# Cross-attention and routed FFN on one core: the last FFN rearranged (half of the output product ahead, ranks from the PSUM bank, keys and queries in two banks, end of the program reordered)

## The chip, the cores and the metric

The kernel runs on one core of a Trainium2 chip. The metric is the device time of one execution in microseconds. Three executions of the kernel before gave 905.43, 905.71 and 909.38 us; their median is 905.71 us. A further execution was recorded with the hardware profiler: 908.64 us, of which 906.5 us are the span from its first to its last instruction. All times inside the span below are counted from the span's start in that one execution.

The engines are named as in the profile: PE is TensorE (matmuls), PEld its weight loads, DVE is VectorE, ACT is ScalarE, POOL is GpSimd, SP is SyncE. Each engine runs its own instruction list in order, and engines meet at semaphores.

## The reference

```python
B, S, D = 8, 512, 256                      # samples, tokens, width; context of 1024 tokens; 16 heads of 16
x = x + cross_attention(layernorm(x), ctx, mask)          # ends with  out @ w_o.T
y = layernorm(x)
scores = y @ w_router
idx = top_k(scores, 128)                                  # 128 of the 512 tokens of each sample
x_sel = y[idx]
h = rmsnorm(x_sel, g1);  q, k, v = split(h @ W_qkv.T)     # 16 heads of 16
x_attn = causal_softmax(q k^T / 4) v @ W_out.T
h2 = rmsnorm(x_sel + x_attn, g2)
x_ff = (silu(h2 @ W1.T) * (h2 @ W2.T)) @ W3.T             # inner width 682
out = x + y.at[idx].set(x_sel + x_attn + x_ff)
```

The output is therefore `x + y` for every row, and for the 128 chosen rows `x_attn + x_ff` is added on top.

## The kernel before

The eight samples are a software pipeline. In the loop over `b`, each of the 32 steps (`STEPS`) of sample `b` is one pair of score products, one pair of exponentials on ACT and one set of value products; the FFN of sample `b - 1` and the projections of sample `b + 1` are put between the steps by tables (`PE_SLOT`, `ACT_SLOT`, `DVE_ORDER`). All of these use one PSUM bank, `MISC` (7), for everything that is not attention.

The FFN of the last sample has nothing to hide behind. It runs after the loops, by the lists `PE_FFN`, `ACT_FFN`, `DVE_FFN` and `POOL_FFN`, with its PSUM banks from `BANK_LAST`. It is one dependent chain that crosses the engines. In order: `wo0`, `wo1` (output product of cross-attention, PE; residual sum and layernorm statistics, DVE), `var` (POOL: reciprocal root of the variance), `y` (DVE: four normalised tiles, then four scores), `spread` (PE lays the 512 scores along every partition; ACT copies them to `all_scores` in SBUF), `rank0` to `rank3` (DVE counts for each token how many scores lie ahead of it and builds the selection matrix `sel`), `gather` (PE multiplies `sel` with `y`; DVE takes the rows, squares them, scales them by POOL's `rms0`), `hidT` (PE transposes, ACT copies), `kq` and `v` (PE; DVE and ACT copy), `fs` (scores, PE; exponentials, ACT), `causal` (POOL), `pv`, `wout`, `hid2T`, then `u0`, `w0`, `u1`, `w1` (four products of 48 matmul records each, with ACT's tanh and DVE's two multiplications per half), and `down:0`, `down:1` with DVE's last sum `att`. POOL's stage `add` (L775 to L784) then adds the 128 rows to the output in DRAM with one indirect DMA.

Between the stages of this chain PE is given products that nobody reads, `spare_products`, in the numbers of `SPARE` (L88): they multiply the constant bf16 tile `before` with 512 columns and write an unused bank. They stand in PE's list ahead of the stage that they are named after, so that stage's matmuls can start only when its spare products are through.

`base = x1 + y` (L674) is made by DVE after `gather`, and SP stores it (L242). POOL's `add` waits for that store (L779) because it adds onto it. A `check` of all denominators of the softmaxes goes into `checks`; PE sums it over the partitions (`flag`), and DVE turns it into `flags_i`. Two operations of that check (L980 to L985) stand between `y` and `rank0` in DVE's list.

The program has two blocks. The first ends when all five engines have arrived (the profile puts these instructions at L803). SP arrives only after `wait_ge(added, 16 * B)` (L858), and POOL only after waiting for the last indirect DMA (L783). In the second block, whose body runs only if the check failed, each engine loads `flags_i`, branches over the body, and meets the others once more (L1071); with that the program ends.

## Time and profile before

| what | value |
|---|---|
| median of 3 executions (lowest, highest) | 905.71 us (905.43, 909.38) |
| profiled execution | 908.64 us |
| its span | 906.5 us |
| PE busy | 868.0 us (96%), 12039 matmul records |
| ACT busy | 570.1 us (63%) |
| DVE busy | 317.3 us (35%) |
| POOL busy | 93.1 us (10%) |
| mean granted TensorE clock | 0.995 of full speed |

Shares over the span tell of the seven steady rounds. The change lies in the last 70 us, where each engine mostly waits for another one, so the table's shares say little about it; the order of events in time is what is to be read. PE's busy time there also holds the spare products.

### The profile page before, as it was taken

The numbers are of one execution on the slowest core, as the hardware profiler recorded it, in microseconds if no ns is written. First come the engines' busy times: TensorE is split into PE (matmuls) and PEld (weight loads), VectorE is DVE, ScalarE is ACT, GpSimd is POOL, SyncE is SP. The second block draws the span as 40 slices with busy tenths as digits, with TensorE's granted clock in tenths as the row PEclk, the third lists the DMA queues.
The fourth block names the chain that finished last, engine by engine and source line by source line (L and its number), as shares of the span: only waits on it lengthen the run. The fifth ranks groups of instructions, "written<-read, shape, count | busy, mean of one in ns | idle before, by whom it ended". The sixth has DMA issues, their size and how long they took to land. (4 is left out here: it accounts for less than half of the span.)

```text
span 906.5 us, 28692 instructions
## 1 busy us (share of the span) xinstructions
PE 868.0 (96%) x12039; PEld 304.9 (34%) x12039; DVE 317.3 (35%) x919; ACT 570.1 (63%) x645; POOL 93.1 (10%) x147
## 2 busy tenths in 40 slices
PE   7999999999999999999999999999999999999974
PEld 2322232333333423334323433334323432323443
DVE  3122126331553217331453316442363314421631
ACT  3566767666676767666676666766676667776010
POOL 4000101110100101011000101011101100010010
PEclk9999999999999999999999999999999999999998
DMA  5060200120011200111001200101001000100000
GB/s 180 32 209 1 77 3 25 49 77 8 3 33 40 78 8 25 48 56 28 5 25 49 78 7 25 49 17 63 8 2 48 31 8 2 48 2 9 1 24 9
DMA packets 25226, 33.73 MB, mean 37 GB/s; under 512 B 1246, under 2 KB 22024, under 8 KB 25096
## 3 DMA queue, kind: packets, MB, share of 16 engines
q1 hardware_dynamic: 23944, 30.81, 10.6%
q0 software_dynamic: 1152, 1.05, 1.0%
q8 instruction: 98, 1.61, 0.7%
q14 instruction: 32, 0.26, 0.1%
HBM read 26.61 MB, written 5.24 MB: 35 GB/s over the span
## 5 line engine op out<-in xcount | busy, mean ns | idle before, releaser
L470 ACT ACTIVATE probs<-pair_bank 128x1024 f32<-128x1024 f32 x512 | 496.2, 1021 | 237.7 <-ACTq L469 237.7
L440 PE MATMUL pair_bank<-q_sb,k_sb 32*64 32x512 f32 x4096 | 285.9, 613 | 8.6 <-PEq L437 8.5
L459 PE MATMUL o_bank<-probs,va 128*32 128x512 f32 x2048 | 272.9, 604 | 1.4 <-ACT probs L470 1.1
L459 PEld LDWEIGHTS o_bank<-probs,va 128*32 128x32 f32 x2048 | 41.5, 108 | 205.1 <-issue 116.4
L440 PEld LDWEIGHTS pair_bank<-q_sb,k_sb 32*64 32x64 f32 x4096 | 61.0, 130 | 141.2 <-issue 141.2
L543 DVE STREAM_TRANSPOSE o_blk<-o_bank 128x512 f32<-128x512 f32 x32 | 22.9, 717 | 138.2 <-DVEq L542 138.2
L256 PE MATMUL m_bank<-wv_sb,ctx_in 128*32 128x256 f32 x1024 | 61.5, 380 | 0.0
L256 PE MATMUL m_bank<-ctx_in,wk_sb 128*32 128x512 f32 x480 | 60.3, 592 | 0.0
L585 DVE TENSOR_SCALAR va<-m_bank,valid 128x256 f32<-128x256 f32 x64 | 28.1, 479 | 63.6 <-DVEq L582 63.4
L256 PEld LDWEIGHTS m_bank<-hid_t,w 128*32 128x32 f32 x1392 | 39.3, 110 | 17.3 <-issue 16.7
L256 PEld LDWEIGHTS m_bank<-wv_sb,ctx_in 128*32 128x32 f32 x1024 | 33.1, 110 | 34.6 <-issue 19.3
L256 PE MATMUL m_bank<-hid_t,w 128*32 128x128 f32 x1392 | 43.4, 273 | 0.5 <-PEq L271 0.5
L266 PE MATMUL o_bank<-before 128*128 128x512 bf16 x120 | 30.7, 414 | 2.7 <-POOL before L864 2.7
L256 PE MATMUL m_bank<-xn_t,wq_sb 128*32 128x512 f32 x240 | 29.6, 592 | 0.0
L772 POOL TENSOR_SCALAR_AFFINE_SELECT p_f<-p_f 128x1024 f32<-128x1024 f32 x16 | 17.5, 1091 | 116.4 <-POOLq L770 115.3
L756 POOL TENSOR_TENSOR mask_in<-mask_in,mask_row 128x256 int32<-128x256 int32 x32 | 22.4, 729 | 68.4 <-POOLq L753 68.4
L781 POOL DMA_INDIRECT out_dram<-att,row_of x8 | 13.3, 1668 | 152.2 <-POOLq L780 152.2
L596 DVE TENSOR_SCALAR q_sb<-m_bank,parity 128x512 f32<-128x512 f32 x15 | 11.3, 750 | 47.1 <-DVEq L595 47.1
L256 PEld LDWEIGHTS m_bank<-ctx_in,wk_sb 128*32 128x32 f32 x480 | 15.7, 110 | 35.9 <-issue 35.9
L616 DVE TENSOR_TENSOR x<-x,m_bank 128x512 f32<-128x512 f32 x14 | 9.6, 687 | 50.9 <-DVEq L615 50.9
L789 POOL TENSOR_SCALAR ms<-ms 128x1 f32<-128x1 f32 x16 | 3.1, 191 | 235.6 <-POOLq L788 235.6
L256 PE MATMUL m_bank<-wo,o_t 128*32 128x256 f32 x448 | 26.7, 379 | 0.0
(166 smaller groups left out, 623.8 us busy)
## 6 DMA issues: line engine op xcount, KB each, us to landing
ctx_in<-in_ctxT SPq DMA_DIRECT2D x7, 1024.0 KB, 5.0
x_in<-in_x SPq DMA_DIRECT2D x8, 512.0 KB, 4.0
x<-in_x SPq DMA_DIRECT2D x8, 512.0 KB, 4.4
mask_in<-in_mask SPq DMA_DIRECT2D x8, 512.0 KB, 3.9
out_dram<-base SPq DMA_DIRECT2D x8, 512.0 KB, 5.3
ctx_in<-in_ctxT SPq DMA_DIRECT2D x2, 512.0 KB, 7.1
mask_row<-in_mask SPq DMA_DIRECT2D x8, 128.0 KB, 3.9
wqkv<-in_wqkvT SPq DMA_DIRECT2D x1, 768.0 KB
```

The lines of the kernel that those rows point to most:

```text
L256: last = nc.tensor.matmul(dst[j], a[:, j], c, start=(begins and n == 0), stop=(ends and n == len(pairs) - 1))
L266: last = nc.tensor.matmul(dst, before[:, 0, 0:P], before[:, 1], start=True, stop=True)
L440: last = nc.tensor.matmul(pair_bank[pairs[r // 2]][j:j + 64, r % 2], key_tile(b, s, r)[:, j:j + 64], query_tile(b, s, r), start=True, stop ...
L459: last = nc.tensor.matmul(o_bank[32 * r:32 * r + 32], va[b % 2][:, t, HV * h:HV * h + 32], probs[s % 2][:, r], start=(t == 0), stop=(t == ...
L470: nc.scalar.activation(probs[s % 2][:, 2 * e:2 * e + 2, :], pair_bank[p][:], ACT.Exp, scale=HD ** -0.5).then_inc(s_free[p], 1)
L543: nc.vector.transpose(o_blk[:], o_bank[:]).then_inc(o_free, 1)
L585: last = nc.vector.tensor_scalar(by_head(va[b % 2][:, t])[:, :, 0:HD], bank[i][:, e * D:(e + 1) * D].rearrange("p (h d) -> p h d", h=H), o ...
L596: nc.vector.tensor_scalar(q_sb[b % 2][:, m, 0], bank[i], parity[:, 0:1], None, ALU.mult).then_inc(q_sb_ready, 1)
L616: nc.vector.tensor_tensor(x1[:, 2 * pr:2 * pr + 2], x1[:, 2 * pr:2 * pr + 2], bank[i].rearrange("p (t d) -> p t d", t=2), ALU.add).then_in ...
L756: last = nc.gpsimd.tensor_tensor(mask_words[:, t * WORDS:(t + 1) * WORDS], mask_words[:, t * WORDS:(t + 1) * WORDS], first, ALU.subtract)
L772: last = nc.gpsimd.affine_select(out=half, in_=half, compare_op=ALU.is_ge, fill=0.0, base=0, pattern=[[0, H8], [1, CAP]], channel_multipli ...
L781: nc.gpsimd.indirect_dma_start(out.rearrange("b s d -> (b s) d"), bass.IndirectOffsetOnAxis(row_of[:, 0:1], 0), att[:], None, compute_op=A ...
```

## The change

The lists of the last FFN are rewritten and six things change.

1. `wo`: the output product of the last sample is made in four banks, one for each tile of 128 tokens. Its first half (the heads whose transposed output `o_t[:, 0]` is there early) runs before the last attention group is normalised, the second half after. DVE adds each tile as it comes. `SPARE` ahead of it falls from 12 to 2, and these go to bank 4.
2. `y` becomes `score`: the mean is subtracted while POOL makes the reciprocal root; the scores are made with the root as the scalar factor; `y` itself is multiplied with the root after the scores have been handed on.
3. `spread` goes to bank 4, and `rank0` to `rank3` read it there. ACT's copy to `all_scores` is gone from this FFN. `SPARE` falls from 24 to 15 ahead of `spread` and from 36 to 25 ahead of `gather`.
4. The check of the denominators moves behind `gather` on DVE (`check all`), and `base` behind the keys and queries, so the store is issued later.
5. `k,q`: keys go to one bank and queries to the next, so DVE can take the keys while PE makes the queries. `u1` is put ahead of `w0`.
6. The end: POOL waits for `base_stored` before `delta_ready`, and no longer for its own last indirect DMA; SP's wait for `added` moves from the end of the first block to the second block, behind the load of `flags_i`.

```diff
-BANK_LAST = {"wo0": 0, "wo1": 1, "spread": 7, "gather": 0, "hidT": 7, "kq": 0, "v": 1, "pv": 7, "wout": 0,
+BANK_LAST = {"wo": 0, "spread": 4, "rank0": 4, "rank1": 4, "rank2": 4, "rank3": 4, "gather": 0, "hidT": 7, "k,q": 0, "v": 7, "pv": 7, "wout": 0,
...
-PE_FFN = ["wo0", "wo1", "spread", "gather", "hidT", "kq", "v", "fs", "pv", "wout", "hid2T", "flag", "u0", "w0", "u1",
+PE_FFN = ["wo", "spread", "gather", "hidT", "k,q", "v", "fs", "pv", "wout", "hid2T", "flag", "u0", "u1", "w0",
           "w1", "down:0", "down:1"]
-ACT_FFN = ["spread", "hidT", "v", "fs", "hid2T", "u0", "u1"]
-DVE_FFN = ["wo0", "wo1", "y", "rank0", "rank1", "rank2", "rank3", "gather", "base", "kq", "pv", "wout", "check", "u0", "w0", "u1", "w1",
+ACT_FFN = ["hidT", "v", "fs", "hid2T", "u0", "u1"]
+DVE_FFN = ["wo", "score", "rank0", "rank1", "rank2", "rank3", "gather", "check all", "k,q", "base", "pv", "wout", "check", "u0", "u1", "w0", "w1",
...
-SPARE = {"wo0": 12, "spread": 24, "gather": 36, "hidT": 10, "pv": 14, "wout": 6, "hid2T": 10}
+SPARE = {"wo": 2, "spread": 15, "gather": 25, "hidT": 10, "pv": 14, "wout": 6, "hid2T": 10}
...
         def pe_ffn(pe, stage, i, part=None):
+            if stage == "wo":
+                pe.wait_ge(o_t_ready, 1)
+                tiles = [take_bank(pe, i + t)[:, 0:D] for t in range(QT)]
+                for t in range(QT):
+                    product(tiles[t], [(o_t[:, 0, t * P:(t + 1) * P], wo[:, 0])], ends=False)
+                pe.wait_ge(o_t_ready, 2)
+                pe.sem_inc(o_t_ready, -2)
+                for t in range(QT):
+                    product(tiles[t], [(o_t[:, 1, t * P:(t + 1) * P], wo[:, 1])], begins=False).then_inc(done["wo"], 1)
...
+            elif stage == "k,q":
+                pe.wait_ge(hidT_sb, 1)
+                pe.sem_inc(hidT_sb, -1)
+                for e in range(2):
+                    dst = take_bank(pe, i + e)
+                    for n in range(2):
+                        first = (D if e == 0 else 0) + n * P
+                        last = product(dst[:, n * CAP:(n + 1) * CAP],
+                                       [(wqkv[:, c, first:first + P], hid_t[:, c]) for c in range(KC)])
+                    last.then_inc(done["kq"], 1)
...
         def dve_ffn(dve, stage, b, i):
+            if stage == "wo":
+                dve.wait_ge(xres_in, 16)
+                dve.sem_inc(xres_in, -16)
+                for t in range(QT):
+                    dve.wait_ge(done["wo"], 1)
+                    dve.sem_inc(done["wo"], -1)
+                    nc.vector.tensor_tensor(x1[:, t], x1[:, t], bank[i + t][:, 0:D], ALU.add).then_inc(bank_free[i + t], 1)
+                    dve.drain()
+                    nc.vector.bn_stats(stats2[:, t], x1[:, t])
+                dve.drain()
+                for t in range(QT):
+                    nc.vector.bn_aggr(mv2[:, t], stats2[:, t])
+                dve.drain().then_inc(var2_ready, 1)
+            elif stage == "score":
+                for t in range(QT):
+                    nc.vector.tensor_scalar(y[:, t], x1[:, t], mv2[:, t, 0:1], None, ALU.subtract)
+                dve.wait_ge(rstd2_ready, 1)
+                dve.sem_inc(rstd2_ready, -1)
+                dve.drain()
+                for t in range(QT):
+                    unused = ties[t // 2][:, (t % 2) * D:(t % 2 + 1) * D]
+                    nc.vector.scalar_tensor_tensor(out=unused, in0=y[:, t], scalar=rstd2[:, t:t + 1], in1=wr_b[:], op0=ALU.mult,
+                                                   op1=ALU.mult, accum_out=score[:, t:t + 1])
+                dve.drain().then_inc(score_ready, 1)
+                for t in range(QT):
+                    nc.vector.tensor_scalar(y[:, t], y[:, t], rstd2[:, t:t + 1], None, ALU.mult)
...
             elif stage in ("rank0", "rank1", "rank2", "rank3"):
                 t = int(stage[4])
-                if t == 0:
+                others = all_scores[:] if i == MISC else bank[i]
+                if t == 0 and i == MISC:
                     dve.wait_ge(all_ready, 1)
                     dve.sem_inc(all_ready, -1)
+                elif t == 0:
+                    dve.wait_ge(done["spread"], 1)
+                    dve.sem_inc(done["spread"], -1)
...
+                    if i != MISC:
+                        dve.sem_inc(bank_free[i], 1)
...
+            elif stage == "k,q":
+                dve.wait_ge(done["kq"], 1)
+                dve.sem_inc(done["kq"], -1)
+                nc.vector.tensor_copy(k_f[:], bank[i][:, 0:D].rearrange("p (m k) -> p m k", m=M2)).then_inc(bank_free[i], 1)
+                dve.wait_ge(done["kq"], 1)
+                dve.sem_inc(done["kq"], -1)
...
+            elif stage == "check all":
+                nc.vector.tensor_scalar(ties[0][:], inv_all[:].rearrange("p n c -> p (n c)"), DEN_LOW, None, ALU.is_ge)
+                dve.drain()
+                nc.vector.scalar_tensor_tensor(out=ties[0][:], in0=inv_all[:].rearrange("p n c -> p (n c)"), scalar=DEN_HIGH,
+                                               in1=ties[0][:], op0=ALU.is_le, op1=ALU.mult, accum_out=checks[:, 0:1])
+                dve.wait_ge(mask_free, 1)
+                nc.vector.tensor_reduce(checks[:, 1:2], differs[:], op=ALU.add, axis=AX.X)
...
             elif stage == "add":
+                pool.wait_ge(base_stored, 16)
+                pool.sem_inc(base_stored, -16)
                 pool.wait_ge(delta_ready, 1)
                 pool.sem_inc(delta_ready, -1)
-                pool.wait_ge(base_stored, 16)
-                pool.sem_inc(base_stored, -16)
                 nc.gpsimd.indirect_dma_start(out.rearrange("b s d -> (b s) d"), bass.IndirectOffsetOnAxis(row_of[:, 0:1], 0),
                                              att[:], None, compute_op=ALU.add).then_inc(added, 16)
-                pool.wait_ge(added, 16 * (n + 1))
-                pool.sem_inc(add_done, 1)
+                if n != B - 1:
+                    pool.wait_ge(added, 16 * (n + 1))
+                    pool.sem_inc(add_done, 1)
...
                 store(sp, B - 1)
-                sp.wait_ge(added, 16 * B)
...
                 general = sp.value_load(flags_i[0:1, 0:1], min_val=0, max_val=1)
+                sp.wait_ge(added, 16 * B)
                 with sp.If(general == 1):
...
                 with pool.If(general == 1):
+                    pool.wait_ge(added, 16 * B)
+                    pool.sem_inc(add_done, 1)
```

## Rows read from the trace of the kernel before

**Rows 1.** By stretch: length; busy of PE, PEld, DVE, ACT, POOL; PE clock; DMA.

```profile
837.00:896.00 59.00, 48.95 (x610) 26.59 (x602) 25.68 (x78) 5.38 (x10) 4.92 (x8) 0.97 0.03 10
```

**Rows 2.** Timeline, output product to statistics: start us, length us, engine, line, operation.

```profile
839.51 0.71 DVE L552 STREAM_TRANSPOSE o_t<-o_nrm 128x512 f32<-128x512 f32 x1
840.53 3.66 PE L256 MATMUL pair_bank<-wo,o_t 128*32 128x256 f32 x64
842.63 0.69 DVE L616 TENSOR_TENSOR x<-x,pair_bank 128x512 f32<-128x512 f32 x1 [2.41 <-DVEq L615]
843.41 0.75 DVE L620 BATCH_NORM_STATS2 stats<-x 128x6 f32<-128x256 f32 x2
...
845.96 0.38 DVE L624 BATCH_NORM_AGGREGATE mv<-stats 128x2 f32<-128x6 f32 x4
...
847.04 1.05 POOL L766 TENSOR_TENSOR rstd<-veps,neg_half 128x4 f32<-128x4 f32 x1 [0.24 <-issue]
```

**Rows 3.** Timeline, normalisation, scores, spread and ranks.

```profile
848.23 1.38 DVE L630 TENSOR_SCALAR y_tok<-x,mv,rstd 128x256 f32<-128x256 f32 x4 [1.90 <-DVEq L628]
849.69 0.43 DVE L634 SCALAR_TENSOR_TENSOR ties<-y_tok,wr_b 128x256 f32<-128x256 f32 x1
...
851.49 0.62 PE L247 MATMUL m_bank<-ident,score 128*128 128x128 f32 x4 [2.02 <-PEq L271]
...
852.24 0.60 ACT L497 ACTIVATE all_scores<-m_bank 128x512 f32<-128x512 f32 x1 [14.63 <-ACTq L496]
...
853.03 0.35 DVE L644 SCALAR_TENSOR_TENSOR ties<-all_scores,score,before 128x128 f32<-128x128 f32 x1 [0.43 <-DVEq L641]
...
857.82 0.77 DVE L606 TENSOR_SCALAR sel<-iota_r,rank 128x128 f32<-128x128 f32 x2
```

**Rows 4.** Groups by form on DVE, one operation from SBUF and one from PSUM: count, busy us, mean ns.

```profile
L647 DVE SCALAR_TENSOR_TENSOR ties<-all_scores,score,before 128x384 f32<-128x384 f32 x1 | 0.6, 617 | 0.0
...
L717 DVE SCALAR_TENSOR_TENSOR silu<-half_tanh,pair_bank 128x384 f32<-128x384 f32 x1 | 0.6, 555 | 1.4 <-DVEq L716 1.4
```

**Rows 5.** Timeline of PE: spare products ahead of spread, ahead of gather, and gather.

```profile
844.12 5.35 PE L266 MATMUL o_bank<-before 128*128 128x512 bf16 x24
...
851.95 9.62 PE L266 MATMUL o_bank<-before 128*128 128x512 bf16 x36
861.50 1.95 PE L256 MATMUL pair_bank<-y_tok,sel 128*32 128x257 f32 x32
```

**Rows 6.** Busy time by stretches of 1 us around the ranks, columns as in Rows 1.

```profile
852.00:853.00 1.00, 1.00 (x7) 0.38 (x5) 0.60 (x3) 0.60 (x1) 0.00 (x0) 0.83 0.00 0
853.00:854.00 1.00, 1.00 (x4) 0.42 (x3) 0.97 (x4) 0.00 (x0) 0.00 (x0) 0.50 0.00 0
...
856.00:857.00 1.00, 1.00 (x6) 0.49 (x5) 0.93 (x6) 0.00 (x0) 0.00 (x0) 0.97 0.00 0
```

**Rows 7.** Timeline, base, keys and queries.

```profile
866.39 1.23 DVE L674 TENSOR_TENSOR base<-x,y_tok 128x1024 f32<-128x1024 f32 x1
...
867.85 1.96 PE L256 MATMUL pair_bank<-hid_t,wqkv 128*32 128x128 f32 x64 [0.84 <-PEq L271]
...
869.97 0.42 DVE L680 COPY k_f<-pair_bank 128x256 f32<-128x256 f32 x1 [2.36 <-DVEq L679]
870.32 0.87 DVE L682 TENSOR_SCALAR q_f<-pair_bank,parity 128x256 f32<-128x256 f32 x2
```

**Rows 8.** Timeline of PE, rest of the four inner products.

```profile
889.45 3.15 PE L256 MATMUL pair_bank<-hid_t,w 128*32 128x128 f32 x107 [0.78 <-issue]
```

**Rows 9.** Timeline, the last sum and the indirect DMA.

```profile
895.52 0.42 DVE L739 TENSOR_TENSOR att<-att,pair_bank 128x256 f32<-128x256 f32 x1 [1.87 <-DVEq L738]
...
896.89 1.66 POOL L781 DMA_INDIRECT out_dram<-att,row_of  x1 [12.97 <-POOLq L780]
```

**Rows 10.** DMA issues after 895 us: engine, count, us to landing.

```profile
out_dram<-att,row_of POOLq DMA_INDIRECT x1, 3.8
```

**Rows 11.** Waits of SP's queue at the end: total us, times, longest.

```profile
SPq L1071 <- PEq L1071: 4.3, 1, 4.3
```

More of the change, by code:

```diff
@@ L676, in dve_ffn @@
                 dve.drain().then_inc(base_ready, 1)
+            elif stage == "k,q":
[4 more added lines that the diff above has]
+                dve.sem_inc(done["kq"], -1)
+                for par in range(2):
+                    last = nc.vector.tensor_scalar(q_f[:, :, par], bank[i + 1][:, 0:D].rearrange("p (m k) -> p m k", m=M2),
+                                                   parity[:, par:par + 1], None, ALU.mult)
+                last.then_inc(bank_free[i + 1], 1)
+                dve.drain().then_inc(kq_sb, 1)
             elif stage == "kq":
@@ L976, in _ @@
                 dve.drain()
[L977 to L987 removed]
+                for stage in DVE_FFN:
                     dve_ffn(dve, stage, B - 1, BANK_LAST.get(stage, MISC))
@@ L1060, in _ @@
                     if stage in SPARE:
-                        spare_products(SPARE[stage], bank[1] if stage == "wo0" else o_bank[:])
+                        spare_products(SPARE[stage], bank[4] if stage == "wo" else o_bank[:])
                     if stage == "fs":
```

19 lines of the change are left out of this document (4 added, 15 removed).

## The prediction

> **What bounds the kernel now.** I read the busy time by stretch first, then the timeline of the last 70 us engine by engine, and last what happens behind the last computing instruction. The stretch from 837 to 896 us is 59 us long and no engine but PE is near full: DVE is busy for 26 us, ACT and POOL for 5 us each [rows 1]. PE's 49 us hold 112 spare products that nobody reads. So nothing is bound by throughput here; the time is the length of one dependent chain, and only three kinds of thing shorten it: a link that is taken off the chain, a link that starts on part of its input, and a queue (PE's spare products above all) that no longer keeps a ready link waiting. The seven steady rounds before 837 us keep their instructions, except that POOL waits for two old semaphores in the other order; I cost them at nothing.
>
> The links, with their ends: the last transposed group `o_t` is there at 839.51 + 0.71 = 840.22, the output product runs from 840.53 to 844.19, DVE's first sum starts at 842.63, the statistics end at 845.96 + 0.38 = 846.34, POOL's root at 847.04 + 1.05 = 848.09 [rows 2]. Then come `y` from 848.23, the scores from 849.69, `spread` on PE at 851.49, ACT's copy at 852.24, the ranks from 853.03 to 857.82 + 0.77 = 858.59 [rows 3]. And here the chain leaves DVE: `gather` could follow 0.3 us behind its input, as the output product follows `o_t` [rows 2], so at 858.9, but it starts at 861.50, when the 36 spare products ahead of it are through [rows 5]. That is 2.6 us in which PE's own filling is the bound.
>
> **Part 1, output product (gain 0.9 us).** The first half (32 of 64 records, 3.66 / 2 = 1.83 us) goes ahead of `o_t`'s second half. A spare product takes 5.35 / 24 = 0.22 us [rows 5]; the 12 of before took 2.7 us ahead of 840.5, so PE is free from about 837.8. Two remain, then five waits of the queue; starting at about 838.4 the half ends at 840.3, just as `o_t` comes. If it were late, each 0.1 us would cost 0.1 us. From 840.5 each tile takes 0.46 us. DVE's first sum, before 2.1 us behind the start of the product [rows 2], now comes 0.46 + 0.3 us behind it, at 841.25. The load moves to DVE: a 256-wide sum is 0.42 us (the sum of `att` [rows 9]), a gap of 0.09 us as between the 512-wide sum and the statistics, 0.38 us for one tile's statistics [rows 2], and some 0.05 us for the wait: 0.93 us a tile, longer than PE's 0.46. Four tiles end at 845.0, so the statistics are complete at 845.45 instead of 846.34. Bounds: 0.7 us (0.1 us more per wait) to 1.1 us. POOL then ends at 847.2.
>
> **Part 2, mean and root apart (gain 1.45 us).** The four subtractions (1.38 us [rows 3]) run from 845.5 to 846.9, beside POOL's root, which ends at 847.2: they are covered. Without that cover they would cost up to 1.38 us again. The scores start at 847.35 and take 1.47 us as before (849.69 to 851.16), so `spread` starts near 849.15 instead of 851.49. Together with part 1 that is 2.35 us.
>
> **Part 3, ranks from the bank (gain 0.25 us).** Removed: ACT's copy with its two hand-overs, from the end of `spread` at 852.11 to 853.03, 0.9 us [rows 3]. Now `spread` ends at 849.8, and DVE could start at 850.05. But the multiplication of `y` by the root (1.38 us plus drain) sits ahead of `rank0` in DVE's queue and ends at 850.3; behind it wait the ranks, and everything behind them. So the ranks start at 850.45: 1.3 us behind `spread`'s start where it was 1.54. The two check operations that stood at this place were hidden behind ACT before and now stand behind `gather`, beside POOL's root, PE's `hidT` and the key product; they take 0.43 + 0.69 + 0.15 us by their shapes, and the `base` operation of 1.23 us that stood in this place was hidden as well [rows 7]. The eight counting operations now read PSUM. A 384-wide three-operand operation from SBUF took 617 ns, one from PSUM 555 ns [rows 4], so I charge nothing; bounds -0.3 to +0.5 us over the eight. The Trainium skill ("VectorE: DVE Perf Modes", the errata section) speaks against this edit: it gives VectorE 58 fixed cycles from SBUF and 120 from PSUM at 0.96 GHz, which by an estimate from that page would cost 8 x 65 ns = 0.5 us. The rows here show no such step, and the measurement decides. The ranks end at 850.45 + 5.56 = 856.0, 2.6 us earlier than before.
>
> **Part 4, fewer spare products (gain 2.2 us).** The clock: after PE's idle stretch from 849.47 (end of the 24 products) to 851.49 the granted clock fell to half at about 852.7 and came back at about 856.0; four products fitted into a microsecond instead of six to seven [rows 5, 6]. In the changed kernel PE has 15 spare products (3.3 us) behind the output product, which ends at 842.4, and is then idle from about 845.9 to 849.15, 3.2 us instead of 2.0: I expect the fall again, earlier. 25 products at full clock are 5.4 us, from 849.6 to 855.0; with 3.3 us of them at half clock it is 1.7 us more, 856.7. `gather` may start at 856.3. So the bound is DVE or PE by a little: I take 856.7, between 856.3 and 857.2 (the last if the half clock lasts longer). Before it was 861.50: 4.8 us in all, of which 2.6 are parts 1 to 3 and 2.2 this one.
>
> **Part 5, keys and queries (gain 0.35 us).** The product of keys and queries is 64 records, 867.85 to 869.81, 0.84 us for each half [rows 7]. DVE's copy of the keys (0.42 us, its next operation 0.35 us behind it) started at 869.97, behind the whole; now it runs beside the second half, and the queries can start at 869.97 instead of 870.32. The later `base` (1.23 us) is beside PE's scores, ACT's exponentials, POOL's masking and the value product, all ahead of DVE's next input. The store goes out 4 us later and has over 15 us left before POOL needs it; its queue on SP has nothing behind it. Bounds 0.2 to 0.4 us.
>
> **Part 6, inner products (gain 0.1 us).** PE is the bound here; 0.78 us of it is a stall inside `w0` that no wait explains [rows 8]. The other order lets DVE finish its last gate sooner, which took at most 0.2 us from PE. The Trainium skill ("Runtime: NRT & Kernel Launch", the section on instruction fetch) says that a sequencer's instructions come in blocks of 256; by that the stall would be a late block, and with 60 PE instructions fewer ahead of it, it would fall 60 instructions later, still among these products. From the rows alone I keep it, with -0.8 to +0.8 us as its bounds.
>
> **Part 7, the end (gain 2.25 us).** The last sum ends at 895.94, POOL issues from 896.89 to 898.55 [rows 9], the DMA lands 3.8 us after 896.89, at 900.7 [rows 10], and only then does the first block close; the second block takes the rest to 906.5, 5.8 us, of which SP stands 4.3 us waiting for PE's queue [rows 11]. With both waits for the DMA gone from the first block, it closes behind the issue, 900.7 - 898.55 = 2.15 us earlier. SP's wait for the landing, about 2 us behind the new close, is then hidden behind its 4.3 us of waiting for PE. The swapped waits of POOL take one wait from between 895.94 and 896.89: 0.1 us, bounds 0 and 0.2.
>
> **The sum** against the profiled execution: 0.9 + 1.45 + 0.25 + 2.2 + 0.35 + 0.1 + 2.25 = 7.5 us, 908.64 - 7.5 = 901.1. The profiled execution is 2.9 us above the median of the three timed ones. One part of the sum may be missing from these: without the fall of the clock the 36 products would end 1.7 us earlier, part 4 would shrink to 0.5 us and the sum to 5.8. No row tells how many of the timed runs had it. I go between the two, 6.8 us: 905.71 - 6.8 = 898.9.
>
> **Rivals.**
> (a) POOL's instruction list can't close the block before its DMA has left or landed. For it: no row of before shows POOL doing anything behind this DMA without an explicit wait. Against it: the engine shows 1.66 us for the DMA and no more [rows 9]. It takes back 2.15 us: 901.1.
> (b) Before's timed runs had no clock fall, and the new ones have one that makes PE late: sum 5.8 - 0.6 = 5.2 us, 900.5. For it: 2.9 us between profile and median.
> (c) Part of the chain does not shorten, because DVE is now its carrier from 841 to 856 us: 0.1 us more at each of the four tile waits, 0.5 us for PSUM reads, and a stall of 0.8 us that comes twice or at the branch into the second block. Together some 2 us: 900.9. The branch target lies elsewhere in the instruction list than before, and its price could change either way.
> (d) Slower. The longer idle of PE (3.2 us) puts the clock to half and it stays there, since the chain behind gives PE only short pieces. Three of PE's links behind the ranks, the gather (1.95 us), keys and queries (1.96 us) and the four inner products (192 records at 3.15 / 107 us, 5.65 us), are 9.5 us at full clock [rows 5, 7, 8]; at half clock these alone cost 9.5 us more, and the result would be 905.71 - 6.8 + 9.5 = 908.4 or above. It ends slower from the point where the half clock covers more than 6.8 us of these links. Against it: after the fall in the rows the clock returned within 3.3 us under spare products, and 25 of them follow here too [rows 6].
> (e) The change doesn't do what it says: the halves do not overlap, since the first half stands behind five waits, and PE's products, not DVE, set when the tiles come; then part 1 is 0.3 us and the rest stands: 899.5, inside the range.
>
> **How the numbers follow.** The forecast with its near variants, (e) among them (897 to 900.2), has 0.62; (a) 0.12; (b) and (c) together 0.17; more gain than the sum, down to 896, 0.04; (d) 0.02; and 0.03 for a mishap that leaves within 0.5%. A measurement of this kernel can tell about 0.5%, 4.5 us, from no change: faster means below 901.2. Of (a), (b) and (c) some three quarters stay below it. That gives faster 0.89, same 0.08, slower 0.03. The range holds the forecast, and (a) to (c) with their own spread: 896.3 to 902.3.
>
> **What would show it.** In the changed profile: the statistics complete near 845.45, `spread` at 849.15, the first count at 850.45 with no ACT copy ahead of it, the last selection at 856.0, `gather` within 0.6 us of it, the half clock before 854; `q_f` starting right at the end of the product; POOL's DMA near 891.5; and the span ending 7.5 us behind POOL's start instead of 9.6 (906.5 - 896.9). Part 3 is wrong if the counts are longer than 617 ns at 384 wide; part 4 if spare products still run when the ranks are done; part 7 if the distance from POOL's DMA to the end stays at 9.6 us. The whole is wrong if the granted clock is half beyond the gather.

## The result and the profile after

The changed kernel takes 902.68 us (median of 9 executions, 901.19 to 903.85). The kernel before, executed beside it, takes 907.67 us (median of 9, 905.43 to 909.38). The ratio is 0.9944, with a 95% interval of 0.9932 to 0.9957: faster by 5.0 us, or 0.56%. The forecast was 898.9 us with a range of 896.3 to 902.3. So the direction was right, the time lies outside the range, and 1.8 us of the forecast gain of 6.8 us did not come. The other 2.0 us between 898.9 and 902.68 are the level that the forecast started from: three executions of the kernel before had given 905.71, nine give 907.67.

The two profiled executions are 908.64 and 902.56 us, with spans of 906.5 and 900.6 us. To compare them I count from the moment at which the last transposed group `o_t` is complete, 840.22 us before [rows 2] and 839.03 + 0.71 = 839.74 in the changed kernel. That removes 0.48 us that came from the unchanged rounds. In the twelve traces of this study, whose rounds have the same instructions, this moment lies between 839.64 and 841.02 us, so the rounds alone move an execution by over a microsecond.

The timeline of the changed kernel; columns as in [rows 2]:

```profile
839.03 0.71 DVE L572 STREAM_TRANSPOSE o_t<-o_nrm 128x512 f32<-128x512 f32 x1
...
844.23 0.38 DVE L640 BATCH_NORM_AGGREGATE mv<-stats 128x2 f32<-128x6 f32 x4
...
844.78 1.14 DVE L645 TENSOR_SCALAR y_tok<-x,mv 128x256 f32<-128x256 f32 x4 [0.17 <-issue]
844.85 0.38 POOL L836 TENSOR_SCALAR veps<-mv 128x4 f32<-128x4 f32 x1 [11.17 <-POOLq L835]
845.46 1.11 POOL L838 TENSOR_TENSOR rstd<-veps,neg_half 128x4 f32<-128x4 f32 x1 [0.24 <-issue]
846.76 0.49 DVE L651 SCALAR_TENSOR_TENSOR ties<-y_tok,rstd,wr_b 128x256 f32<-128x256 f32 x1 [0.84 <-DVEq L647]
...
848.81 0.62 PE L247 MATMUL pair_bank<-ident,score 128*128 128x128 f32 x4 [3.64 <-PEq L271]
...
849.27 7.25 PE L266 MATMUL o_bank<-before 128*128 128x512 bf16 x25
849.92 0.35 DVE L696 SCALAR_TENSOR_TENSOR ties<-pair_bank,score,before 128x128 f32<-128x128 f32 x1 [0.18 <-DVEq L693]
...
854.71 0.77 DVE L626 TENSOR_SCALAR sel<-iota_r,rank 128x128 f32<-128x128 f32 x2
...
856.44 1.95 PE L256 MATMUL pair_bank<-y_tok,sel 128*32 128x257 f32 x32
...
864.92 0.88 DVE L738 TENSOR_SCALAR q_f<-pair_bank,parity 128x256 f32<-128x256 f32 x2 [0.45 <-DVEq L736]
...
891.18 1.66 POOL L853 DMA_INDIRECT out_dram<-att,row_of  x1 [12.64 <-POOLq L852]
```

In distances from `o_t`, with the gain summed up to each link:

| link | before | changed | gain so far | forecast |
|---|---|---|---|---|
| statistics complete | 6.12 | 4.87 | 1.25 | 0.9 |
| POOL's root | 7.87 | 6.83 | 1.04 | 0.9 |
| `spread` starts | 11.27 | 9.07 | 2.20 | 2.35 |
| ranks start | 12.81 | 10.18 | 2.63 | 2.6 |
| ranks end | 18.37 | 15.74 | 2.63 | 2.6 |
| `gather` starts | 21.28 | 16.70 | 4.58 | 4.8 |
| `q_f` starts | 30.10 | 25.18 | 4.92 | 5.15 |
| POOL's DMA issue | 56.67 | 51.44 | 5.23 | 5.35 |
| end of the span | 66.28 | 60.86 | 5.42 | 7.5 |

The first link gained 0.35 us more than forecast; from POOL's root down to the last but one line the forecast holds to a quarter of a microsecond. Then, between POOL's issue and the end, 0.2 us were gained where 2.15 had been expected: 906.5 - 896.9 = 9.6 us before, 900.6 - 891.2 = 9.4 us changed. The place is seen by asking for the instructions of the line at which the first block closes. Columns: line, queue, operation and count; length in ns; start in us. First the changed kernel, then the kernel before:

```profile
L876 SPq DRAIN  x1: 128/128/128, 868.3 to 868.3; - x1
...
L876 POOLq DRAIN  x1: 4222/4222/4222, 890.9 to 890.9; - x1
L876 DVEq DRAIN  x1: 19/19/19, 891.2 to 891.2; - x1
```

```profile
L803 SPq COMPARE_BRANCH  x1: 38/38/38, 900.7 to 900.7; - x1
L803 POOLq DRAIN  x1: 130/130/130, 900.8 to 900.8; - x1
```

At the close of the block every queue has a drain. POOL's was 0.13 us long before, standing behind an explicit wait for the DMA. In the changed kernel it is 4.22 us long and ends at 890.9 + 4.2 = 895.1, and the DMA lands 3.9 us behind its issue at 891.18, at 895.1:

```profile
out_dram<-att,row_of POOLq DMA_INDIRECT x1, 3.9
```

The explicit waits were taken out, and the drain that had always stood behind them does the same waiting.

### The profile page after: what moved, and what is told of

Same layout as the page of the kernel before. It is cut to its first block and busy times, and to the rows that moved or that the text cites. A ratio compares the mean times of both kernels' runs of the same rounds, so it can differ in the third digit from the quotient of the medians.

```text
span 900.6 us, 28635 instructions
## 1 busy us (share of the span) xinstructions
PE 860.4 (96%) x12003; PEld 300.9 (33%) x12009; DVE 318.8 (35%) x925; ACT 569.5 (63%) x644; POOL 93.3 (10%) x147
## 3 DMA queue, kind: packets, MB, share of 16 engines
q0 software_dynamic: 1152, 1.05, 1.0%
## 5 line engine op out<-in xcount | busy, mean ns | idle before, releaser
L266 PE MATMUL o_bank<-before 128*128 128x512 bf16 x95 | 25.7, 426 | 3.3 <-POOL before L936 2.7
```

The costliest lines, as they stand in the source:

```text
L266: last = nc.tensor.matmul(dst, before[:, 0, 0:P], before[:, 1], start=True, stop=True)
```

## The experiments

Times below are medians; each kernel was timed beside the kernel before, and "ratio" is to that, with its 95% interval. The kernel before itself had medians of 907.67 us beside the changed kernel, 907.42 beside four experiments (the end put back, the DMA behind the first block, 30 spare products, 25 in the kernel before), 906.72 beside four others (ranks from the copy, mean and root together, keys and queries in one bank, both edits together) and 906.55 beside the last two (the second DMA, scores before the root). So a distance to the changed kernel can differ by up to 1.1 us between medians and ratios, and a total that differs by less than that shows nothing by itself; the traces then have to carry the reading. Distances are from `o_t`, as above.

**The end put back.** In the changed kernel, only the waits of part 7 put back (POOL's two waits ahead of the DMA stay swapped):

```diff
-                if n != B - 1:
-                    pool.wait_ge(added, 16 * (n + 1))
-                    pool.sem_inc(add_done, 1)
+                pool.wait_ge(added, 16 * (n + 1))
+                pool.sem_inc(add_done, 1)
...
                 store(sp, B - 1)
+                sp.wait_ge(added, 16 * B)
...
-                sp.wait_ge(added, 16 * B)
                 with sp.If(general == 1):
...
-                    pool.wait_ge(added, 16 * B)
-                    pool.sem_inc(add_done, 1)
```

> The changed kernel with its end put back: POOL waits for its last indirect DMA again and SP's wait for it stands in the first block. Theory T (in the changed kernel the closing drain on POOL waits for the DMA's landing, 4.2 us long in the trace, so taking out the explicit waits bought nothing): the distance from POOL's DMA issue to the end of the span is 9.4 to 9.7 us, as in both kernels so far (9.57 before, 9.38 changed), and the time is that of the changed kernel, 902.7, within 0.5 us. POOL's drain is short again, 0.2 us or less, and stands behind the landing. Rival R1 (removing the waits did save 2 us, and something else in the second block took it back, such as a longer branch): the distance grows to 11.4 us or more and the time to about 904.8.

Measured: 902.47 us (901.79 to 904.99, 6 executions), ratio 0.9949 (0.9931 to 0.9967), beside 902.68 for the changed kernel. From POOL's issue at 890.68 to the end at 900.4 it is 9.7 us, 0.3 us more than in the changed kernel. The drain is short again and stands behind the landing:

```profile
L875 POOLq DRAIN  x1: 130/130/130, 894.6 to 894.6; - x1
```

So theory T holds: taking the waits out, as part 7 does, is worth 0.2 to 0.3 us in the traces and nothing that can be timed, and the second block took nothing back.

**The DMA behind the first block.** If the drain of the first block is what waits, the DMA must be issued behind it.

```diff
-                for stage in POOL_FFN:
+                for stage in POOL_FFN[:-1]:
                     pool_ffn(pool, stage, B - 1)
...
+                pool_ffn(pool, "add", B - 1)
                 general = pool.value_load(flags_i[0:1, 0:1], min_val=0, max_val=1)
```

> The changed kernel with POOL's last stage (its two waits and the indirect DMA) moved behind the meeting of the first block, ahead of POOL's load of the flag. Theory T: the first block now closes when DVE has written the flag, about 1.3 us behind the last sum; the DMA is issued there, 1.66 us, and lands 3.9 us after its start, while the other engines load the flag and branch, 5.1 to 5.4 us. The end then comes about 5.3 us behind DVE's last drain instead of 9.4 us behind POOL's issue: 3.6 to 4.0 us less than the changed kernel, near 898.9. POOL's drain at the end of the second block shows the wait for the landing. Rival R1 (the second block has a price of its own for whatever runs beside it): at most 1 us less, 901.7 or above.

Measured: 899.1 us (898.59 to 899.9, 6 executions), ratio 0.9908 (0.9892 to 0.9924). Its slowest execution is below the fastest of the changed kernel (901.19); the medians differ by 3.6 us, the lower end of what was expected. The timeline, then the drain of the second block and SP's waits (us in total, times, longest):

```profile
892.68 1.66 POOL L853 DMA_INDIRECT out_dram<-att,row_of  x1 [13.21 <-POOLq L852]
```

```profile
L1133 POOLq DRAIN  x1: 2870/2870/2870, 893.7 to 893.7; - x1
...
L1133 PEldq DRAIN  x1: 79/79/79, 896.8 to 896.8; - x1
```

```profile
SPq L1223 <- DMA out_dram<-att,row_of: 4.0, 1, 4.0
SPq L1133 <- PEq L1133: 0.4, 1, 0.4
```

The DMA is issued 1.1 us later behind the last sum than in the changed kernel, and still the end comes 4.5 us behind the issue instead of 9.4. POOL's drain ends at 893.7 + 2.9 = 896.6, the DMA lands at 892.68 + 3.9 = 896.6, and PE's drain, behind its branch, stands at 896.8. The two waits now lie beside each other and end together: SP waits 4.0 us for the DMA and then only 0.4 us for PE, where it had waited 4.3 us for PE alone [rows 11].

**A second DMA in front of the drain.** The same trace pattern would come from a drain that waits a fixed time behind an issue. A load of 512 KB into a buffer that is no longer read is put on POOL's queue behind the indirect DMA:

```diff
+                if n == B - 1:
+                    pool.dma_start(x_in[:], io["x"][0].rearrange("(t p) d -> p t d", p=P)).then_inc(extra_in, 16)
                 if n != B - 1:
                     pool.wait_ge(added, 16 * (n + 1))
...
                 sp.wait_ge(added, 16 * B)
+                sp.wait_ge(extra_in, 16)
```

> The changed kernel with one more transfer on POOL's queue behind the indirect DMA: a load of 512 KB (one sample of x) into the buffer x_in, which nobody reads; only SP waits for it, in the second block. Theory T1 (POOL's closing drain waits until every DMA that POOL issued has landed): the drain grows from 4.2 us to some 3 us more, by the issue of the load and its own landing, and ends within 0.1 us of the later landing; the whole end moves by the same amount. Theory T2 (the drain waits a fixed time behind an issue, or for the indirect form alone): the drain ends where the indirect DMA lands, or 3.9 us behind the last issue whatever lands when.

Measured: 905.27 us (904.36 to 905.81, 8 executions), ratio 0.9985 (0.9973 to 0.9997): 2.6 us above the changed kernel. In the trace the end comes 903.0 - 890.6 = 12.4 us behind the indirect DMA's issue instead of 9.4. Timeline, landings, and the drain:

```profile
890.64 1.65 POOL L854 DMA_INDIRECT out_dram<-att,row_of  x1 [11.89 <-POOLq L853]
891.73 1.45 POOL L857 DMA_DIRECT2D x_in<-in_x  x1
```

```profile
x_in<-in_x POOLq DMA_DIRECT2D x1, 512.0 KB, 5.5
out_dram<-att,row_of POOLq DMA_INDIRECT x1, 3.9
```

```profile
L879 SPq DRAIN  x1: 130/130/130, 868.6 to 868.6; - x1
...
L879 POOLq DRAIN  x1: 6422/6422/6422, 891.0 to 891.0; - x1
```

The indirect DMA lands at 894.5 and the load at 897.2. The drain ends at 891.0 + 6.4 = 897.4: with the later landing to 0.2 us (the expectation said 0.1, and the rounding of these rows can hide 0.1), 2.9 us behind the first one, and 5.7 us behind the last issue instead of 3.9. T1 holds, for a plain load too; T2 falls. SP's drain is different: in the changed kernel it stands at 868.3 us and is 0.13 us long, right behind the store that SP issued at 867.91 and that took 3.0 us to land, until 870.9. It did not wait for its DMA.

**30 spare products ahead of the spread.** The changed kernel with `"spread": 30` in `SPARE` instead of 15.

> The changed kernel with 30 spare products instead of 15 ahead of the spread stage, so PE is filled from 842 to about 848.4 us and idle for 0.5 us instead of 3.6. If the half clock in the ranks comes from that idle stretch: the granted clock stays at full speed from 840 to 880 us, the 25 products ahead of the gather end near 854.6, and the gather starts 0.3 to 0.4 us behind the last selection instead of 1.0 us; the time is 0.5 to 0.6 us below the changed kernel, 902.1. If the fall has another cause, the clock is at half somewhere between 849 and 856 us and gather and time stay. If the 30 products reach into the spread, it starts later and the time rises by what they reach.

Measured: 901.77 us (901.35 to 902.58, 6 executions), ratio 0.9938 (0.9922 to 0.9954), 0.9 us below the changed kernel; the executions of the two overlap. The mechanism is plain in the traces. The granted clock stands behind POOL's busy time (columns: stretch; length; busy of PE, PEld, DVE, ACT, POOL; PE clock; DMA share; GB/s). The changed kernel, then the one with 30:

```profile
849.00:850.00 1.00, 1.00 (x8) 0.64 (x7) 0.81 (x4) 0.00 (x0) 0.00 (x0) 0.96 0.00 0
850.00:851.00 1.00, 1.00 (x4) 0.33 (x3) 0.95 (x4) 0.00 (x0) 0.00 (x0) 0.50 0.00 0
...
853.00:854.00 1.00, 1.00 (x6) 0.37 (x5) 0.93 (x6) 0.00 (x0) 0.00 (x0) 0.83 0.00 0
```

```profile
850.00:851.00 1.00, 1.00 (x6) 0.44 (x5) 1.00 (x4) 0.00 (x0) 0.00 (x0) 1.00 0.00 0
```

```profile
842.03 6.42 PE L266 MATMUL o_bank<-before 128*128 128x512 bf16 x29 [0.16 <-issue]
...
855.85 1.95 PE L256 MATMUL pair_bank<-y_tok,sel 128*32 128x257 f32 x32 [0.99 <-PEq L271]
```

With PE filled up to 848.45 there is no half clock at all, the 25 products ahead of the gather end early, PE idles for 0.99 us, and the gather starts at a distance of 16.06 us, right behind the ranks; in the changed kernel it starts at 16.70, directly behind spare products. So the half clock of the changed kernel comes from its own idle stretch of 3.64 us ahead of the spread: in all three traces with 30 products ahead of the spread it is gone.

**How long the half clock lasts.** The kernel with the DMA moved has the same PE list up to the gather as the changed kernel. Its trace:

```profile
848.00:849.00 1.00, 0.30 (x2) 0.33 (x3) 0.88 (x4) 0.00 (x0) 0.00 (x0) 0.50 0.00 0
...
853.00:854.00 1.00, 1.00 (x4) 0.45 (x3) 0.93 (x6) 0.00 (x0) 0.00 (x0) 0.50 0.00 0
```

```profile
849.58 7.86 PE L266 MATMUL o_bank<-before 128*128 128x512 bf16 x25
857.37 1.29 PE L256 MATMUL pair_bank<-y_tok,sel 128*32 128x257 f32 x20
```

Here the clock is at half from about 847.4 to 854.2 us, 6.8 us instead of 3.4, and the gather starts at a distance of 17.73. What decides between the two lengths no run shows. Of the seven traces of kernels with 15 products ahead of the spread, four show 3.4 us at half clock and three 6.8 us, with the gather at 16.5 to 16.9 us or at 17.7 to 18.7 us. The two clearest neighbours, the changed kernel (16.70) and this one (17.73), differ by 1.0 us there and up to there by nothing in their instructions. Both kernels with 24 ahead of it (the kernel before and the next experiment) show 3.4 us.

**Only the products ahead of the gather, in the kernel before.** `"gather": 25` instead of 36, nothing else.

> The kernel before with 25 instead of 36 spare products ahead of the gather, nothing else. If these products are what the gather waited for (it started 2.9 us behind the last selection): it starts within 0.4 us of the selection at full clock or about 1 us with a clock fall, and the time is 2.0 to 2.6 us below the kernel before, near 905.3. If only runs with a clock fall had that wait, the gain over the timed runs is nearer 1 us: 906.6.

Measured: 905.76 us (904.33 to 908.45, 12 executions), ratio 0.9979 (0.9967 to 0.9991), so 1.7 us by the medians and 1.9 us by the ratio. In the trace, which has the clock fall, the gather starts at a distance of 18.90 us instead of 21.28, 2.4 us earlier:

```profile
857.36 0.77 DVE L606 TENSOR_SCALAR sel<-iota_r,rank 128x128 f32<-128x128 f32 x2
...
858.66 1.95 PE L256 MATMUL pair_bank<-y_tok,sel 128*32 128x257 f32 x32
```

It is 0.5 us behind the last selection, where it was 2.9 us [rows 3, 5]. These products were what the gather waited for; this one number in a table is over a third of the whole gain.

**Ranks from the copy.** The changed kernel with the spread in bank 7 and the ranks on ACT's copy in SBUF:

```diff
-             "spread": 4, "rank0": 4, "rank1": 4, "rank2": 4, "rank3": 4,
+             "spread": 7,
...
-ACT_FFN = ["hidT", "v", "fs", "hid2T", "u0", "u1"]
+ACT_FFN = ["spread", "hidT", "v", "fs", "hid2T", "u0", "u1"]
```

> The changed kernel with the ranks on ACT's copy of the scores in SBUF again (spread to bank 7, copy by ACT), all else as changed. If reading PSUM costs a counting operation nothing: the eight operations have the same lengths to 10 ns (384 wide: 617 to 619 ns), the ranks take 5.56 us from first to last either way, and they start 1.5 us behind the start of the spread instead of 1.1, so 0.4 us later. If PSUM cost 65 ns an operation, the ranks here would be 0.5 us shorter and the two would cancel. In the total: 0.1 to 0.5 us slower than the changed kernel, as the spare products ahead of the gather hide most of it in runs with the clock fall.

Measured: 903.02 us (901.65 to 903.86, 6 executions), ratio 0.9957 (0.9942 to 0.9973), 0.3 us above the changed kernel, within what the executions scatter (1.2 us by the ratios, whose intervals meet). In its trace the ranks start 1.99 us behind the start of the spread (1.11 in the changed kernel) and take 5.56 us from SBUF, where they take 5.56 us from PSUM (849.92 to 855.48). The edit is worth 0.9 us ahead of the ranks, more than the 0.25 us of the sum, partly because the half clock of this execution began with the spread and made it longer. Most of it is given back at the gather, which spare products hold in the changed kernel (16.94 against 16.70 us). The Trainium skill ("VectorE: DVE Perf Modes", the errata section) would, by the estimate in the prediction, make the eight operations 0.5 us longer from PSUM than from SBUF; this pair of traces shows no difference.

**Mean and root together again.** The changed kernel with the stage `y` in place of `score` (`DVE_FFN = ["wo", "y", ...`).

> The changed kernel with the stage y as before in place of score: mean and root in one operation behind POOL's root, scores after it with the constant 1.0 as factor. Theory: the chain from the end of the statistics to the spread gets 1.38 us of normalising back and gives back two smaller losses of the new form, the three-operand operation with a factor from memory (0.48 us each in the changed trace against 0.42 us) and POOL's work beside DVE's subtractions (its first operation 0.38 us against 0.23 us). So spread starts about 1.0 us later relative to the statistics' end, POOL's first operation is 0.23 us again, and the time is 0.7 to 1.0 us above the changed kernel, 903.5. If POOL's 0.38 us came from anything else, it stays at 0.38 us.

Measured: 903.94 us (902.88 to 905.95, 10 executions), ratio 0.9968 (0.9956 to 0.9981), 1.3 us above the changed kernel, where 0.7 to 1.0 were expected; its trace has the half clock of 6.8 us. Spread starts at a distance of 10.01 us instead of 9.07: part 2 is worth 0.94 us, not 1.45. Both suspected losses are there. POOL's first operation is short again:

```profile
845.56 0.23 POOL L836 TENSOR_SCALAR veps<-mv 128x4 f32<-128x4 f32 x1 [11.16 <-POOLq L835]
846.02 1.05 POOL L838 TENSOR_TENSOR rstd<-veps,neg_half 128x4 f32<-128x4 f32 x1 [0.24 <-issue]
```

0.23 and 1.05 us here, 0.38 and 1.11 us in the changed kernel, where DVE's subtractions run at the same time. The three-operand operation with the factor 1.0 is 0.42 us long again, and 0.49 us with the factor from memory.

**Keys and queries in one bank again.** The changed kernel with the stage `kq` in both lists.

> The changed kernel with keys and queries in one bank again, all else as changed. From the start of that product to the start of the score product the traces give 3.83 us before and 3.50 us changed; here it should be 3.8 us, and the time 0.3 us above the changed kernel, which three rounds can hardly tell from none. If the gain had come from base standing behind instead of ahead of it, the distance stays at 3.5 us.

Measured: 902.7 us (902.25 to 904.27, 5 executions), ratio 0.9958 (0.9941 to 0.9976): no difference to the changed kernel in the median, and none by the ratio that is clear of the intervals. In the trace the score product starts 3.83 us behind the start of the key and query product, as in the kernel before (867.85 to 871.68); in the changed kernel it is 866.30 - 862.80 = 3.50. Part 5 is worth 0.33 us; it is seen in the trace and not in the time.

**Both edits that paid, together.** DMA behind the first block, and 30 spare products ahead of the spread.

> Both edits that paid, together: the indirect DMA behind the first block and 30 spare products ahead of the spread. They act at different places (855 us and 891 us), so they should add: in the trace full clock from the output product to the end of the last product, gather 0.3 to 0.4 us behind the last selection, the span's end 4.4 to 4.6 us behind POOL's issue. Time 0.7 to 0.9 us below the one with the DMA moved alone (899.1), 898.3. If the second block's price depends on what ran before it, they don't add and the time stays near 899.

Measured: 899.25 us (897.69 to 899.64, 5 executions), ratio 0.9912 (0.9893 to 0.993), against 899.1 for the moved DMA alone. In the total the 0.7 to 0.9 us did not show. In the trace they did: from `o_t` to the end it is 56.58 us, against 57.56 with the DMA alone and 60.86 in the changed kernel; but this execution reached `o_t` at 841.02 instead of 839.64 us. The mean granted clock is 0.998 or 0.999 in four of the five executions, against 0.995 to 0.997 with the DMA alone, which suggests that the half clock is gone in these too. Whether the time follows is open; five and six executions can't tell it from the 1.4 us by which the rounds differ.

**Scores before the root.** On top of the last one, the scores are made from the tiles with the mean subtracted while POOL makes the root, and only the 128x4 scores are multiplied by it:

```diff
+                dve.drain()
+                for t in range(QT):
+                    unused = ties[t // 2][:, (t % 2) * D:(t % 2 + 1) * D]
+                    nc.vector.scalar_tensor_tensor(out=unused, in0=y[:, t], scalar=1.0, in1=wr_b[:], op0=ALU.mult,
+                                                   op1=ALU.mult, accum_out=score[:, t:t + 1])
                 dve.wait_ge(rstd2_ready, 1)
                 dve.sem_inc(rstd2_ready, -1)
                 dve.drain()
-                for t in range(QT):
-                    unused = ties[t // 2][:, (t % 2) * D:(t % 2 + 1) * D]
-                    nc.vector.scalar_tensor_tensor(out=unused, in0=y[:, t], scalar=rstd2[:, t:t + 1], in1=wr_b[:], op0=ALU.mult,
-                                                   op1=ALU.mult, accum_out=score[:, t:t + 1])
+                nc.vector.tensor_tensor(score[:], score[:], rstd2[:], ALU.mult)
```

> The kernel with the DMA behind the first block and 30 spare products, and in it the scores made from the tiles with the mean subtracted but without the root, while POOL still makes the root; then one multiplication of the 128x4 scores by the root. In the chain DVE is then busy with subtractions (1.14 us) and scores (1.4 us) until about 2.6 us behind the end of the statistics, 0.65 us behind POOL's root, and the four operations with a factor from memory (1.64 us) are off the chain behind the root, for one small operation of 0.15 us and a drain. Spread starts about 8.15 us behind the last transposed group instead of 9.06: 0.9 us earlier, and with it ranks and gather. PE's 30 spare products end about there, so up to 0.3 us may be lost to them. Time 0.6 to 0.9 us below its base (899.25 by five timed runs, 899.1 for the one without the products): 898.5. If the scores were not on the chain, nothing changes.

Measured: 897.17 us (896.97 to 897.73, 4 executions), ratio 0.9896 (0.9879 to 0.9912). It is the fastest kernel of the study: 5.5 us below the changed kernel and 1.0% below the kernel before. It is also 1.3 us below the 898.5 that were expected, more than the edit explains, as the rows show. The timeline:

```profile
846.53 0.42 DVE L649 SCALAR_TENSOR_TENSOR ties<-y_tok,wr_b 128x256 f32<-128x256 f32 x1
...
848.07 0.16 DVE L654 TENSOR_TENSOR score<-score,rstd 128x4 f32<-128x4 f32 x1
...
848.78 0.60 PE L247 MATMUL pair_bank<-ident,score 128*128 128x128 f32 x4
```

Its `o_t` is complete at 840.28, so the spread starts at a distance of 8.50 us, 0.56 us earlier than with the root as the factor, where 0.9 was expected. The scores were ready at 848.23, and PE starts the spread at 848.78 without having been idle: the 30 spare products now reach into it, 0.25 us of the missing 0.35. The ranks start 0.76 us earlier than in the kernel it was built on, at 9.42 instead of 10.18, and so does the gather (15.30, 16.06). That is what the edit is worth. The two traces differ by 2.6 us in their spans: the rounds give 0.7 us (841.02 against 840.28) and a stall of 0.9 us among the inner products, told of in the last section, is absent in this trace. PE's instruction list is the same in both. So by the traces 0.76 of the 2.6 us belong to the edit; whether the 2.1 us between the medians divide alike is open.

## Why the prediction was right and wrong

**Right: the chain and its first six parts.** To POOL's issue the sum said 5.35 us and the traces show 5.23. The links that the prediction named as next late were the ones: DVE from 841 to 850 us, `y`'s multiplication ahead of the ranks (it ends at 849.74 and the ranks start at 849.92, a distance of 10.18 us; behind the end of the spread at 849.43 and the forecast's hand-over of 0.25 us it would be 9.9), PE's spare products ahead of the gather.

**Part 1** was put at 0.9 us and is 1.25. A tile takes 0.84 us on DVE and not 0.93: the wait between two tiles costs nothing, since the next sum follows 0.35 us behind the start of the statistics, and PE's second half started 0.15 us behind `o_t` instead of 0.3. In the code the waits for the banks stand ahead of it now; that they are the reason no run shows.

**Part 2** was put at 1.45 us and is 0.94. Two terms were left out. The row of an operation with the constant 1.0 was used for one with a factor from memory; the right price stood in the trace, in the 256-wide counting operations (0.48 us). And POOL was taken to be as fast beside DVE's subtractions as alone. Parts 1 and 2 together were put at 2.35 and measured 2.20.

**Part 3**: the price of reading PSUM was put at nothing, and it is nothing (5.56 us both ways). **Part 5**: 0.35 forecast, 0.33 measured. **Part 6**: 9.83 us from the first inner product to the end of the last sum before (886.11 to 895.94), 880.73 to 890.32 = 9.59 us changed; but the stall in it varies from execution to execution (below), so that the 0.1 us of this part can't be told.

**Part 4** was right in its mechanism, 0.25 us too large, and too narrow in its bounds. The fall of the clock came, at 850 us, and the gather was at 856.44, or 856.92 on the start of before, where 856.7 was forecast. The term that was short is the 25 products: at the row's own 5.35 / 24 us each they are 5.6 us, not 5.4. The sign of being wrong, spare products still running when the ranks are done, came true (ranks done at 855.48, products until 856.4), but the forecast's own numbers, 856.0 and 856.7, already had them so. What the bounds missed is that behind the longer idle stretch the half clock is 6.8 us long in some executions. The price is 1.0 us at the gather then. The changed kernel probably pays it in some of its timed executions: its trace, with 3.4 us at half clock, has a mean granted clock of 0.995; 3.4 us more would take off another 1.7 / 900.6 = 0.002; and five of the nine executions have 0.992 or 0.993, with 902.68 to 903.85 us, while the other four have 901.19 to 902.58. That is the likeliest place of the 0.4 us between the 5.4 us of the traces and the 5.0 us of the medians. It is an estimate: a mean does not say where the clock fell. Rival (d) named this chain of causes with a longer duration; the clock always came back before the gather was through.

**Part 7 is the step that failed.** It said that with both explicit waits gone "it closes behind the issue", 2.15 us earlier. Rival (a) named the mechanism, that POOL's list can't close the block before the landing, and got 0.12. Its argument for itself was the correct one: no row of before showed POOL passing this DMA without a wait. Against it stood only the 1.66 us of the issue, which tells nothing of the drain behind it. The drain was in the trace of before, 0.13 us long because it stood behind a wait; a short length there is no price for it without that wait. The first three experiments settle it: putting the waits back changes nothing, moving the DMA behind the block gives 3.6 us, and a second DMA stretches the drain with its landing. With 0.2 us in place of the 2.15 us the sum against the profiled execution is 5.55 us, and the measured distance is 5.42.

**The start of the count.** The forecast took 905.71, the median of three executions, two of which were among the fastest of all that followed. It took into account that some of them might lack the clock's fall; the traces add that the rounds ahead of `o_t` alone scatter by 1.4 us, and nine executions have their median at 907.67. Rival (b), that before's timed executions had no fall, is borne out in part. Both traces of kernels with 24 products ahead of the spread have the fall, and so have all seven with 15. But in the profiled execution of before the clock is at half for 3.4 us in the ranks and again from 900.4 us to the end, which makes its mean 0.995; without the first it would be 0.997. Of the 48 executions of the kernel before that were timed beside the experiments, 12 have 0.997, and they take 905.03 to 906.56 us (median 905.8); the 27 with 0.995 or less have a median of 908.1. So a part of before's executions, probably the two lowest of the first three among them, had no fall, and most had one. The means don't say where the clock fell, and no trace of an execution with 0.997 was kept, so this too is an estimate. It makes the level that the forecast started from a matter of which executions three draws happened to hold.

## What to carry to other kernels

A wait that is taken out saves only what nothing behind it repeats: look for the next point at which the same queue must be empty, a block's closing drain above all, and put the transfer behind that point instead of taking its wait away. In a chain across engines, count from a fixed event of the trace and not from the start of the span, and read every filler instruction as something that stands in front of the next real one; the number that fits shifts as soon as a link moves. Take the price of an operation from a row with the same kinds of operands, and with the same neighbour running.

## What the hardware showed unexpectedly

POOL's drain waits until the DMAs issued from POOL have landed (4.22 us for one, 6.42 us for two, 2.87 us in the second block), while SP's drain behind its store was 0.13 us long.

POOL slows down beside DVE: its 128x4 operation took 0.38 us while DVE's 256-wide subtractions ran and 0.23 us without them, its second 1.11 and 1.05 us. The Trainium skill ("SBUF — State Buffer", the section on its two separate sides) describes a port pair that DVE's fast two-port operations and POOL lock against each other; that agrees with the two traces, which show neither the lock itself nor in which mode DVE's subtractions ran.

The stall among the inner products, where there is one, has a fixed place in the instruction list and a variable length. Before, PE stops after 48 + 35 = 83 records of these products [rows 8]; with 11 spare products fewer after 94; in the changed kernel, with 30 fewer, after 111; with 15 of them put back after 96. Each spare product fewer moves it by one record, up to the few waits that were added:

```profile
882.03 1.95 PE L256 MATMUL pair_bank<-hid_t,w 128*32 128x128 f32 x63
...
884.71 2.45 PE L256 MATMUL pair_bank<-hid_t,w 128*32 128x128 f32 x81 [0.72 <-issue]
```

Its length was 0.78 us before, 0.72 here, 0.19 in the kernel with the end put back, 0.89 in the one with both edits; in the one with `kq`, the one with the second DMA and the one with the scores before the root the 144 records run through without it. Two totals can differ by 0.9 us by this alone. The Trainium skill ("Runtime: NRT & Kernel Launch", the section on instruction fetch) says that instructions come in blocks of 256; a fixed place that shifts with the count of instructions agrees with that. The rows show no instruction fetch, so the cause stays open.
